# Second routing of a two-expert mixture kernel in groups of two row tiles, with the first expert weights loaded and split during it

## The reference

```python
x = x + 0.5 * _L0_ffn_ref(_layernorm(x, axis=-1), gate, w0, w1, wo)
x = x + _L0_attn_ref(_layernorm(x, axis=-1), ...)
x = x + 0.5 * _L0_ffn_ref(_layernorm(x, axis=-1), gate, w0, w1, wo)
```

```python
gate_logits = jnp.einsum('bsd,de->bse', x, gate_kernel)
top_k_weights, top_k_indices = jax.lax.top_k(gate_logits, TOP_K)
...
inter = jax.nn.silu(h0) * h1
out = jnp.einsum('bse,bsem,emd->bsd', combine, inter, wo_kernel)
```

## Time and profile before

| what | value |
|---|---|
| time, median of 3 runs (lowest to highest) | 1137.31 us (1135.53 to 1138.65) |
| time of the profiled execution | 1136.86 us |
| its span, first to last instruction | 1135.0 us |
| mean granted PE clock | 0.959 |
| busy in the span: PE, DVE, ACT, POOL | 1012.5, 715.5, 522.4, 444.2 us |
| second routing and what follows up to the first product of the second expert stage | 810.6 to 921.6 us of the span |

### The profile page before, as it was taken

One profiled execution on the slowest core, in us unless ns is written; L12 is line 12 of the kernel. 1 busy time (PEld: TensorE's weight loads), 2 busy tenths in 40 slices (PEclk: granted clock), 3 DMA queues, 4 the chain that ended last, 5 costly groups with the idle time before them and its releaser, 6 DMA issues.

```text
span 1135.0 us, 22156 instructions
## 1 busy us (share of the span) xinstructions
PE 1012.5 (89%) x6200; PEld 810.0 (71%) x6201; DVE 715.5 (63%) x1570; ACT 522.4 (46%) x1127; POOL 444.2 (39%) x401
## 2 busy tenths in 40 slices
PE   5669999998369999999999999999989459999994
PEld 4548788887347777777778777777778448778884
DVE  6365656654457788877887787777344545656542
ACT  2243333422146776767767677777210123433321
POOL 2552233233334553646463644443014422233232
PEclk9999999999669999999999999999999679999998
DMA  9843544532100111111111111111654544544330
GB/s 254 254 166 85 125 101 102 111 50 29 56 1 10 57 38 38 39 29 31 36 38 39 38 39 38 39 38 53 219 162 149 200 128 109 156 106 100 51 55 7
DMA packets 71591, 95.80 MB, mean 84 GB/s; under 512 B 9600, under 2 KB 48640, under 8 KB 71296
## 3 DMA queue, kind: packets, MB, share of 16 engines
q1 hardware_dynamic: 57216, 78.04, 22.6%
q0 software_dynamic: 14304, 16.87, 8.4%
HBM read 64.37 MB, written 34.43 MB: 87 GB/s over the span
## 4 chain that ended last, share of the span: by engine, by line
PE 49%; DMA 27%; issue 11%; POOL 3%; DVE 3%; ACT 1%; POOLq 1%; SPq 0%; DVEq 0%; ACTq 0%
DMA out<-shared,small 13%; DMA x_after_moe<-shared,small 13%; PE bank L1625 10%; PE bank L1652 10%; PE bank L1613 5%; PE bank L1614 5%; PE bank L1615 5%; PE bank L1600 2%; POOL rows_by_expert L533 2%; PE bank L1601 2%; PE bank L1731 1%; PE bank L1568 1%; PE bank L1439 1%; PE bank L1441 1%; PE bank L1443 1%
## 5 line engine op out<-in xcount | busy, mean ns | idle before, releaser
L845 ACT ACTIVATE shared<-bank,small 128x512 f32<-128x512 f32 x256 | 176.5, 690 | 95.2 <-DVE small L1266 94.2
L1266 DVE TENSOR_REDUCE small<-bank 128x1 f32<-128x512 f32 x256 | 174.7, 685 | 47.8 <-PE bank L1615 47.5
L777 ACT CAST split_rows_and_inner<-bank 128x512 fp32r<-128x512 f32 x78 | 46.0, 589 | 246.8 <-PE bank L1424 246.8
L1625 PE MATMUL bank<-constants,shared 128*128 128x128 f32 x1024 | 157.0, 276 | 2.0 <-ACT shared L845 0.5
L1625 PEld LDWEIGHTS bank<-constants,shared 128*128 128x128 f32 x1024 | 123.2, 141 | 44.9 <-issue 14.2
L1441 PE MATMUL bank<-expert_weights_low,split_rows_and_inner 128*128 x312 | 143.5, 460 | 0.0
L1443 PE MATMUL bank<-expert_weights_high,split_rows_and_inner 128*128 x312 | 142.4, 456 | 0.0
L1613 PE MATMUL bank<-expert_weights_high,shared_split 128*128 128x512 f32 x256 | 124.7, 487 | 5.9 <-POOL shared_split L589 5.9
L1439 PE MATMUL bank<-expert_weights_high,split_rows_and_inner 128*128 x312 | 125.2, 401 | 2.9 <-DVE split_rows_and_inner L1075 2.5
L1080 DVE TENSOR_TENSOR split_rows_and_inner<-bank,split_rows_and_inner 128x512 fp32r<-128x512 f32 x78 | 53.9, 691 | 113.7 <-ACT split_rows_and_inner L777 113.7
L546 POOL DMA_INDIRECT out<-shared,small x39 | 61.4, 1574 | 149.4 <-DMA out<-shared,small 120.3
(11 more groups left out here) (187 smaller groups left out, 2120.6 us busy)
## 6 DMA issues: line engine op xcount, KB each, us to landing
expert_weights<-L_ffn_w_kernel SPq DMA_DIRECT2D x32, 512.0 KB, 5.0
shared<-rows_by_expert SPq DMA_DIRECT2D x78, 129.0 KB, 2.1
expert_weights<-L_ffn_wo_kernel SPq DMA_DIRECT2D x16, 512.0 KB, 6.3
shared<-inverse_sums SPq DMA_DIRECT2D x64, 128.0 KB, 2.9
attended_transposed<-shared SPq DMA_DIRECT2D x32, 256.0 KB, 3.0
expert_weights<-x_after_moe SPq DMA_DIRECT2D x8, 512.0 KB, 4.8
expert_weights<-attended_transposed SPq DMA_DIRECT2D x2, 2048.0 KB, 11.2
shared<-attended_transposed SPq DMA_DIRECT2D x2, 2048.0 KB, 10.9
```

What stands on the lines that cost most here:

```text
L845: nc.scalar.activation(prob[k % 4], bank[k % 4][:, :], ACT.Exp, bias=negmax[:, k % 8:k % 8 + 1], accum_out=psum[par][:, hh * GT + qt:hh * ...
L1266: V.tensor_reduce(negmax[:, k % 8:k % 8 + 1], bank[k % 4][:, :], AX.X, ALU.max, negate=True).then_inc(max_ready, 1)
L1625: last = tr(bank[4 + k % 2][:, c * P:(c + 1) * P], prob[k % 4][:, c * P:(c + 1) * P], ident)
```

## The change

The second routing goes in 8 groups of 2 tiles (`GN[1]` = 2). The steps of a group lie differently: PE has the rank products two tiles later than before in group terms (`ranks(1, h - 2)`, `xn_transpose(2, h - 1)` after an even tile, `logits(1, h - 1)` after an odd one), and DVE picks the experts of the group before between the statistics and the normalization of a group. Group x lies in the upper part of the low weights' area, which the attention doesn't use, so SP loads experts 0 and 1 as soon as the output product has read the third group of attended rows (tile 11). ACT and DVE split expert 0 among the steps of the last group. ACT splits expert 1 behind them; DVE does so in the first tile of the expert stage, since the last x group lies where these three pieces go. POOL scatters a group's first copies, takes a root, and scatters its second copies. All helpers get the group's size, which the diff leaves out where it changes only a width.

```diff
+GN = (GT, 2)
...
-        x2group = [late[:, PAIRS * S + k * GT * D:PAIRS * S + (k + 1) * GT * D].rearrange("p (a n) -> p a n", a=GT)
+        x2group = [wlo_plain[:, 2 * B * S + k * GT * D:2 * B * S + (k + 1) * GT * D].rearrange("p (a n) -> p a n", a=GT)
                    for k in range(2)]
...
                 if g > 1:
                     sp.wait_ge(out_stored[g % 2], 16)
-                    sp.wait_ge(xn_ready[2], g - 1)
+                    sp.wait_ge(xn_ready[2], (g - 1) * GT // GN[1])
...
                     load_x(g + 2)
+                elif g + 2 == NG:
+                    sp.wait_ge(wo_psum, (g + 1) * GT)
+                    load_expert(1, 0)
+                    load_expert(1, 1)
             for u in range(2):
                 sp.wait_ge(out_stored[u], 16 * NG // 2)
-            sp.wait_ge(xn_ready[2], NG)
-            load_expert(1, 0)
-            load_expert(1, 1)
             moe(1)
...
-            pool.wait_ge(veps_ready[2], 1)
-            root(2, 0, GT)
-            for g in range(NG):
-                if g + 1 < NG:
-                    pool.wait_ge(veps_ready[2], g + 2)
-                    root(2, 0, GT)
-                scatter(1, g)
+            for g in range(2):
+                pool.wait_ge(veps_ready[2], g + 1)
+                root(2, 0, GN[1])
+            for g in range(NT // GN[1]):
+                scatter(1, g, (0,))
+                if g + 2 < NT // GN[1]:
+                    pool.wait_ge(veps_ready[2], g + 3)
+                    root(2, 0, GN[1])
+                scatter(1, g, (1,))
...
-            for g in range(NG):
+            for g in range(NT // GN[1]):
+                last = g == NT // GN[1] - 1
+                if last:
+                    act.wait_ge(w_in[1], 48 * 2)
+                    split_high(1, 0, 0)
+                    split_high(1, 0, 1)
+                xt_out(2, g, xTr[1], logits_psum[1])
                 copy_rows(1, g)
-                xt_out(2, g, xTr[1], logits_psum[1])
+                if last:
+                    split_high(1, 0, 2)
                 choice_exp(1, g)
+            for piece in range(3):
+                split_high(1, 1, piece)
             moe(1)
...
+                def second_lows():
+                    if f == 1:
+                        for u in range(2):
+                            dve.wait_ge(out_stored[u], 16 * NG // 2)
+                    for piece in range(3):
+                        split_low(f, 1, piece)
...
                     if not is_last(i, k):
                         xt_low(t + 1, (k + 1) % 3)
+                    if f == 1 and is_first(i, k):
+                        second_lows()
                     multiply(t)
...
-            for g in range(NG):
-                x = x2group[g % 2]
-                dve.wait_ge(x_in_sem[g % 2], (g // 2 + 4) * 16)
-                for j in range(GT):
-                    t = g * GT + j
-                    dve.wait_ge(wo_psum, t + 1)
-                    V.tensor_tensor(x[:, j, :], x[:, j, :], bank[5 + j % 2][:, 0:D], ALU.add).then_inc(x2_ready, 1)
-                    second_route(g - 1, j)
-                dve.wait_ge(x2_ready, g * GT + GT)
-                dve.wait_ge(xn_ready[2], g)
-                ln_stats(x, 0, GT, veps_ready[2])
-                dve.wait_ge(rstd_ready[2], g + 1)
-                norm_rows(1, g, x)
-            for part in range(3):
-                second_route(NG - 1, part)
+            half = GN[1]
+            for t in range(NT):
+                h, first = t // half, t % half == 0
+                x = x2group[t // GT % 2]
+                if t % GT == 0:
+                    dve.wait_ge(x_in_sem[t // GT % 2], (t // GT // 2 + 4) * 16)
+                dve.wait_ge(wo_psum, t + 1)
+                j = t % GT
+                V.tensor_tensor(x[:, j, :], x[:, j, :], bank[5 + j % 2][:, 0:D], ALU.add).then_inc(x2_ready, 1)
+                if first:
+                    if h > 1:
+                        find_slots(1, h - 2)
+                    if h > 0:
+                        xt_out(2, h - 1, xTr[1])
+                else:
+                    dve.wait_ge(x2_ready, t + 1)
+                    dve.wait_ge(xn_ready[2], h)
+                    ln_stats(x[:, j - 1:j + 1, :], 0, half, veps_ready[2])
+                    if h > 0:
+                        choose(1, h - 1)
+                    dve.wait_ge(rstd_ready[2], h + 1)
+                    norm_rows(1, h, x[:, j - 1:j + 1, :])
+            end = NT // half - 1
+            split_low(1, 0, 0)
+            xt_out(2, end, xTr[1])
+            find_slots(1, end - 1)
+            split_low(1, 0, 1)
+            choose(1, end)
+            split_low(1, 0, 2)
+            find_slots(1, end)
             tables(1)
             moe(1)
...
+                if t % half == 0:
+                    if h > 1:
+                        ranks(1, h - 2)
+                    if h > 0:
+                        xn_transpose(2, h - 1)
+                elif h > 0:
+                    logits(1, h - 1)
+            end = NT // half - 1
+            xn_transpose(2, end)
+            ranks(1, end - 1)
+            logits(1, end)
+            ranks(1, end)
             counts(1)
             moe(1)
```

More of the change, by code:

```diff
@@ L524, in root, with scatter @@
                                         minus_half[:, 0:count], ALU.pow).then_inc(rstd_ready[n], 1)
-            def scatter(f, g):
+            def scatter(f, g, ks=range(TOPK)):
                 u = g % 3
@@ L530, in scatter @@
                 pool.wait_ge(xn_copied[f], g + 1)
-                for k in range(TOPK):
-                    for j in range(GT):
+                for k in ks:
+                    for j in range(GN[f]):
                         nc.gpsimd.indirect_dma_start(
@@ L796, in step @@
                             split_high(f, e, 2)
-                for e in range(0 if f == 0 else 2):
-                    act.wait_ge(w_in[f], 48 * 2)
-                    for piece in range(3):
-                        split_high(f, e, piece)
                 act.wait_ge(tables_ready[f], 2)
@@ L945, in ln_rows @@
             def ln_rows(n, x, at, g, u):
-                for j in range(GT):
+                for j in range(GN[n // 2]):
                     ins = V.tensor_scalar(rows[u][:, j, 0, 0:D], x[:, j, :],
@@ L962, in choose @@
             def choose(f, g):
-                u = g % 3
+                u, n = g % 3, GN[f]
                 dve.wait_ge(slots_ready[f], g)
                 dve.wait_ge(logits_psum[f], g + 1)
-                own.step(V.tensor_copy(logit.rearrange("p t e -> p (t e)"), bank[2][:, 0:GT * E]))
+                own.step(V.tensor_copy(logit[:, 0:n].rearrange("p t e -> p (t e)"), bank[2][:, 0:n * E]))
                 own.settle()
-                for j in range(GT):
+                for j in range(n):
@@ L970, in choose @@
                     own.step(V.max(top[:, j, :], logit[:, j, :]))
                 own.settle()
-                for j in range(GT):
+                for j in range(n):
                     own.step(V.max_index(topi[:, j, :], top[:, j, :], logit[:, j, :]))
                 own.settle()
-                own.step(V.tensor_copy(topf, topi[:, :, 0:TOPK]))
-                V.tensor_tensor(diff.unsqueeze(2), top[:, :, 1:2], top[:, :, 0:1], ALU.subtract).then_inc(diff_ready[f], 1)
+                own.step(V.tensor_copy(topf[:, 0:n], topi[:, 0:n, 0:TOPK]))
@@ L981, in choose @@
+                own.step(V.tensor_tensor(hot1[:, 0:n], iota_b, topf[:, 0:n, 0:1].to_broadcast([P, n, E]), ALU.is_equal))
+                own.step(V.tensor_tensor(hot2[:, 0:n], iota_b, topf[:, 0:n, 1:2].to_broadcast([P, n, E]), ALU.is_equal))
                 own.settle()
-                V.tensor_tensor(mask, hot1, hot2, ALU.add).then_inc(mask_ready[f], 1)
+                V.tensor_tensor(mask[:, 0:n], hot1[:, 0:n], hot2[:, 0:n], ALU.add).then_inc(mask_ready[f], 1)
+                to = rows[u][:, 0:n, :, :]
@@ L991, in choose @@
+                V.scalar_tensor_tensor(to[:, :, 1, D:D + 1], e2[:, 0:n].unsqueeze(2), 0.5, rden[:, 0:n].unsqueeze(2),
                                        ALU.mult, ALU.mult)
                 for k in range(TOPK):
-                    own.step(V.tensor_copy(rows[u][:, :, k, D + 1:ROW].bitcast(I32),
-                                           ids[:, bass.ds(g * GT, GT)].unsqueeze(2)))
+                    own.step(V.tensor_copy(to[:, :, k, D + 1:ROW].bitcast(I32),
+                                           ids[:, bass.ds(g * n, n)].unsqueeze(2)))
@@ L996, in find_slots @@
             def find_slots(f, g):
[L998 removed]
+                u, n = g % 3, GN[f]
                 dve.wait_ge(ranks_psum[f], g + 1)
[L1000 to L1002 removed]
+                own.step(V.tensor_reduce(msum, mask[:, 0:n].rearrange("p t e -> p e t"), AX.X, ALU.add))
@@ L1116, in step @@
                             split_low(f, e, 2)
-                for e in range(2):
+                if f == 0:
                     for piece in range(3):
```

(3 more changed lines are left out.)

105 lines of the change are left out of this document (44 added, 61 removed).

## The result

| kernel | runs | median, us (lowest to highest) | ratio to before, 95% interval |
|---|---|---|---|
| before | 4 | 1137.1 (1135.53 to 1138.65) | |
| changed | 4 | 1127.94 (1126.73 to 1128.36) | 0.992 (0.9904 to 0.9935) |

The change makes the kernel faster by 9.2 us, 0.8%.

The account below looks back on a forecast made before the run. PE was taken as the bound in second routing and expert stage, with a chain through all engines between; -5.4 - 4.4 + 3.45 + 1.7 = -4.65 us gave 1132.2 profiled, 1132.6 as median, range 1128.8 to 1137.5.

Parts of the forecast that it names:

- The routing loop: Second routing up to the last addition: waits and slow stretch removed, some transposes, ranks and small waits added; -5.4 us.
- The allowance of 0.5 us for small waits: Routing loop: DVE's cover is only 0.2 us thick, so PE waits 0.5 us in all over seven turns.
- the removed waits: Routing loop: PE's three waits before the groups' transposes go, 5.26 us by their idle time.
- Rival 2: Routing loop: PE's waits stay, as DVE is late; at 0.76 us a turn no gain, 1137.9 us; chance 0.22.
- The end of the routing: From last addition to first row load: a shorter chain brings the load at 28.0 us instead of 32.5; -4.4 us.
- What ends last: Before the first row load: SP's zero transfers, landed at 27.0 us, end last; the scatters would release it at about 26.3.
- I take its slow clock as in this stretch before: End of the routing: PE idles some 4 us before the last transposes, so its clock was taken as 0.53.
- A choice, an address step and three splits put into the chain take half of that back: End of the routing: these added DVE steps take back half of the about 6 us that halving the group saves.
- SP's last zero transfer: End of the routing: issued at 24.1 us, landed at 27.0, with the row load another 0.94 us later, at 28.0.
- The first tile: First expert tile: three splits stall PE for +3.45 us, and a fall of the clock behind the wait costs +1.7 us.
- Rival 1: Same forecast without the clock's fall in the first tile, or without small waits: 1131.0 us, down to 1129; chance 0.24.
- Rival 3: Chain at the routing's end: expert loads land late and ACT stops it; slower, 1142 us at 30 us of loading; chance 0.09.

Follow-up runs that it names:

- the dose: Changed kernel plus one unused DVE product of 128x1024 in each of the 8 turns, between choice and normalization: 1145.93 us, ratio 1.0011 to the kernel before.
- The repeat: The changed kernel run once more, unaltered, beside later variants on another chip than its first run: 1137.28 us, ratio 0.993 to the kernel before.
- weights alone: Kernel before, groups of four kept, with x's other buffer, early expert loads, expert 0 split in the last group, expert 1 in the first tile: 1149.22 us, ratio 1.0025.
- before with the stall: Kernel before, with only the three low splits of expert 1 moved into the first expert tile: 1148.72 us, ratio 1.0023.
- groups alone: Changed kernel with groups of two only: x's old area, expert loads after the last normalization, all splits ahead of the first tile: 1135.49 us, ratio 0.990 to before.
- all splits behind: Changed kernel with all splits of experts 0 and 1 behind the routing steps, ahead of the first expert tile: 1134.29 us, ratio 0.9893 to before.

## Why the prediction was wrong in size

The sum stood at 1132.2 us for a profiled execution, and 1126.73 was measured. By the segments the 5.5 us are 1.2 in the loop, 2.9 at the end of the routing, 0.4 in the first tile, and 1.0 outside the steps (0.8 ahead of the routing, 0.2 net in the rest of the stage and behind it). That last us lies in parts that the change doesn't touch and belongs to no term of the prediction; without it the time would have been at the edge of the range.

**The routing loop: -5.4 forecast, -6.63 measured.** The mechanism was right. Three terms were mis-sized. The allowance of 0.5 us for small waits was not needed: DVE's cover is 0.15 us a turn as the dose shows (0.2 was forecast), and PE never waited. The ranks take 0.58 us a turn (828.60 to 829.18), not 0.62: 0.24 us over six turns. And the removed waits cost more than their idle time. Output products ahead of the waits, in PE's timeline of the kernel before:

```profile
824.50 3.62 PE L1731 MATMUL bank<-value_out_weights,shared 128*128 128x256 f32 x16
...
843.94 3.62 PE L1731 MATMUL bank<-value_out_weights,expert_weights 128*128 128x256 f32 x16
...
865.36 3.62 PE L1731 MATMUL bank<-value_out_weights,shared 128*128 128x256 f32 x16
```

From these to the transposes behind them are 5.25, 5.54 and 5.31 us, where the next start follows 3.45 us after such a product if nothing waits: 5.75 us in all, not 5.26. Matmuls overlap at their ends, and an idle time counted from a matmul's modelled end leaves that overlap out. Together these are 1.23 us.

**Rival 2, the waits that stay,** didn't happen, but it was close: 0.15 us. The dose turns it on. The loop's gain is then gone, as the rival said, but only at about 1.0 us a turn, not at 0.76, since the gain was larger; the whole kernel is back at the time before.

**The end of the routing: -4.4 forecast, -7.26 measured.** This is the step that failed. What ends last was right; the chain was too long at both of its parts. The end of the counts was put at 14.9 us and came at 13.12 (890.76; the table's 12.95 is the start of that step). "I take its slow clock as in this stretch before" was a guess at the clock behind an idle time, and here it stayed at 1.00 until the ranks. The repeat, where it fell, shows what that is worth: 0.65 us at the counts. The other 1.1 us are DVE's own steps. Against the prediction's list group 6's addresses began 0.4 us sooner than the clock explains (the normalization alone ended 0.25 sooner) and took 1.02 us instead of 1.3, group 7's mask came 1.55 us behind the second split, not 1.7, and the splits, the choice and roundings make up the rest. The last addresses with the counts took 1.51 us, as forecast: the same step took 1.56 for four tiles, so this one hardly gets shorter with the group. "A choice, an address step and three splits put into the chain take half of that back" is refuted for the splits: without them the counts come 0.42 us sooner, since DVE then waits for turned rows, ranks and gate products.

The second part is behind SP's last zero transfer. I put its landing at 2.9 us and 0.94 us of table reads behind it. From the last issue (900.25) to the row load are 2.61 us, 1.9 to the landing and 0.7 behind it. The median of eight landings was taken for that of the last one, which was the shortest here. (In the kernel before, the last one landed in 2.4 us too, for a median of 2.9.) That is 1.2 us; SP's start and issues, 0.25 us slower than forecast, take a fifth of it back. So the step that failed is the length of this chain, 14.9 + 0.94 + 8.3 + 2.9 + 0.94 us in the prediction: 1.8 us too long up to the counts and 1.2 behind the last zero transfer.

**The first tile: +3.45 and +1.7 forecast, +4.78 measured.** Right in cost and mechanism, but that the clock fell was in part luck: the argument was the length of the wait, and the dose has the same wait of 3.31 us and no fall. The stall is +3.28 us (dose against before), the fall 1.50 (changed against dose), and the stage takes up neither. Rival 1, no fall, is what the dose's profile shows. The Trainium skill ("TensorE: Matmul & The Clock Gate", "HAM oscillation — how this bites in real kernels") says that bursts of matmuls separated by waits start slow; the changed kernel, weights alone and before with the stall agree, with 15.29 to 15.31 us, and the dose with 13.79 us doesn't.

**Rival 3, late expert loads,** didn't happen: the loads were issued from 860.77 us on, ACT's first split began at 880.51 without waiting for a transfer, and PE's wait of 3.84 us before the last transposes was ended by DVE's normalization.

**Where the gain comes from.** The group size gives it all (0.990 alone). The weights part is worth nothing here: on the old groups it costs 0.25%, and beside the new ones the stall in the first tile (+4.5 and +4.8) takes more than its earlier row load gives (25.2 and 26.2 for 28.0). By the segments the changed kernel's two profiles take 315.0 and 316.2 us and groups alone 313.1; the runs don't tell the two kernels apart. Why SP's zero transfers start later and lie up to 2.8 us apart at first in groups alone and up to 2.1 in all splits behind, and 1.2 us in the changed kernel, stays open. Gaps of 2.1 us also come among the later ones, in weights alone and in before with the stall. The first gaps in groups alone, all splits behind and the changed kernel all lie beside POOL's last scatters and DVE's tables, so neither is the answer by itself; no run here takes them apart.

## What to carry to other kernels

Before DVE work is moved to a place where "nothing waits", look at who is waited for in the stage where it lands: three splits that were free between the stages cost 3.3 us inside a stage in which PE has no slack, and 4.8 where the clock fell behind them, and what they free is less. In a chain of short steps over several engines, halving the group shortens the steps that grow with it (the copy of the turned rows from 0.69 to 0.42 us) and leaves others as they are (addresses with counts, 1.56 and 1.51); work that fills another engine's gap in that chain costs almost nothing (three splits of 1.15 us: 0.42 us). And a cover of 0.15 us holds as long as the code stays as it is: one more DVE product of 128x1024 a turn (1.15 us) gives all of the gain back. The median landing taken for the last of a group of transfers, a guessed clock and steps rounded up in a chain were off by 2.8 us here, for a gain of 9.2.

## What the runs showed that was not expected

- One instruction order, two profiles: behind an idle time of 3.83 or 3.84 us PE's clock was 0.50 in the one and 1.00 in the other, and a stall of 3.31 us was followed by a fall in three profiles and by none in a fourth. A stall of 2.80 us, in the repeat, was followed by a fall too. The length of a wait doesn't settle it; waits of 0.80 to 1.70 us in the routing loop were not followed by a fall, and the one of 1.92 or 1.93 us was, in all three profiles that have it (weights alone, before with the stall).
- A scatter of 128 rows takes 0.96 us to issue, and 1.1 to 1.97 us in some cases near DVE's splits: three of the last group's eight before, with the splits beside them, and none of the last four in groups alone and all splits behind, where the splits come later. The dose shows that DVE's work does this: in five turns the scatter beside the added product takes 1.81 or 1.82 us, and the same one in the changed kernel 0.96 to 1.00.
- The first of ACT's zero transfers took 2.14 us to issue, with SP issuing one at the same time; the others took 0.34 us.
